# A batch's head in another order: next queries, second values, next keys and the input's transposes moved between half-steps

## The reference

```
x = x + a_alpha * attention(gamma_a * rmsnorm(x) + beta_a)      # 16 heads of width 16, softmax
x = x + f_alpha * (swiglu(gamma_f * rmsnorm(x) + beta_f) @ out_w + out_b)   # 1024 hidden
```

## Time and profile before

| what | value |
|---|---|
| median of 3 runs (lowest, highest) | 949.28 us (947.05, 949.49) |
| the profiled execution's own time | 951.83 us |
| its span, first to last instruction | 950.0 us |
| mean granted clock of PE | 0.985 |
| PE busy | 917.3 us, 97% |
| DVE busy | 746.9 us, 79% |
| ACT busy | 558.1 us, 59% |
| POOL busy | 266.3 us, 28% |

### The profile page before, as it was taken

How to read it: one execution, slowest core, us unless ns; L and a number is a source line. 1 busy time by engine, 2 the same in 40 slices (tenths; PEclk the granted TensorE clock), 3 DMA queues, 4 the chain that set the end, 5 groups by cost and what they waited for, 6 DMA issues and landing times.

```text
span 950.0 us, 19296 instructions
## 1 busy us (share of the span) xinstructions
PE 917.3 (97%) x7128; PEld 671.5 (71%) x7128; DVE 746.9 (79%) x1435; ACT 558.1 (59%) x1162; POOL 266.3 (28%) x255
## 2 busy tenths in 40 slices
PE   6899999999899999999999999999999999999998
PEld 4677777777544677767776786768577777867587
DVE  4798888999788798778778877887797788778253
ACT  5466545544566666566666656665575756566532
POOL 1256432322101032312322322231223223124242
PEclk9999999999999999999999999999999999999999
DMA  9655457443521212132032203303120321120010
GB/s 259 158 136 151 110 146 167 115 119 85 134 87 40 68 65 66 34 106 83 3 91 57 75 13 85 120 6 91 57 74 3 90 68 42 62 63 8 1 29 23
DMA packets 93757, 75.68 MB, mean 80 GB/s; under 512 B 44880, under 2 KB 79768, under 8 KB 93664
## 3 DMA queue, kind: packets, MB, share of 16 engines
q1 hardware_dynamic: 82680, 63.22, 24.2%
q10 hardware_dynamic: 10984, 11.23, 4.4%
HBM read 27.73 MB, written 12.61 MB: 42 GB/s over the span
## 4 chain that ended last, share of the span: by engine, by line
PE 85%; DVE 4%; ACT 3%; SPq 3%; issue 2%; DMA 1%; POOL 1%; ACTq 0%; DVEq 0%; POOLq 0%
PE bank L1405 17%; PE bank L438 17%; PE bank L1118 13%; PE bank L1424 8%; PE bank L1092 8%; PE raw_pair L1026 6%; PE bank L340 3%; PE bank L1410 2%; PE bank L1496 2%; DVE rowmax L1036 1%; PE bank L1668 1%; SPq L929 1%; PE bank L1542 1%; DMA k_stack<-hid 1%; PE bank L1420 1%
## 5 line engine op out<-in xcount | busy, mean ns | idle before, releaser
L1036 DVE TENSOR_REDUCE rowmax<-raw_pair 128x1 f32<-128x512 f32 x488 | 326.1, 684 | 82.3 <-PE raw_pair L1026 80.2
L1107 ACT ACTIVATE probs<-bank 128x512 f32<-128x512 f32 x344 | 197.2, 598 | 126.1 <-PE bank L1092 122.9
L438 PE MATMUL bank<-up_w,xs_part 128*128 128x512 f32 x768 | 199.9, 411 | 6.0 <-POOL xs_part L417 5.9
L1092 PE MATMUL bank<-q_stack,k_stack 50*128 50x512 f32 x480 | 189.1, 410 | 3.7 <-ACT probs L1107 2.2
L1026 PE MATMUL raw_pair<-k_stack,q_stack 48*128 48x512 f32 x456 | 182.0, 412 | 3.3 <-DVE rowmax L1036 2.0
L438 PEld LDWEIGHTS bank<-up_w,xs_part 128*128 128x128 f32 x768 | 139.6, 192 | 40.8 <-POOL xs_part L417 6.9
L1526 POOL TENSOR_TENSOR hid<-scratch,hid 128x512 fp32r<-128x512 f32 x64 | 82.8, 1294 | 227.2 <-ACT hid L1522 227.2
L1107 ACT ACTIVATE third_probs<-bank 128x512 f32<-128x512 f32 x168 | 96.5, 598 | 63.8 <-PE bank L1092 62.4
L1092 PEld LDWEIGHTS bank<-q_stack,k_stack 50*128 50x128 f32 x480 | 85.7, 185 | 39.1 <-ACT probs L1107 18.8
L1405 PE MATMUL bank<-xf_part,gate_w 64*128 64x512 f32 x384 | 112.2, 401 | 1.1 <-DVE xf_part L1288 1.1
L1405 PE MATMUL bank<-xf_part,hidden_w 64*128 64x512 f32 x384 | 111.5, 399 | 0.0
(11 more groups left out here) (215 smaller groups left out, 1646.6 us busy)
## 6 DMA issues: line engine op xcount, KB each, us to landing
q_stack<-hid SPq DMA_DIRECT2D x78, 128.0 KB, 2.8
k_stack<-hid SPq DMA_DIRECT2D x64, 128.0 KB, 3.1
xk<-xT SPq DMA_DIRECT2D x32, 128.0 KB, 3.1
xt<-x_tok SPq DMA_DIRECT2D x32, 128.0 KB, 2.8
x_spill<-x1t ACTq DMA_DIRECT2D x32, 128.0 KB, 2.4
xa_spill<-xa ACTq DMA_DIRECT2D x32, 128.0 KB, 2.3
x_in<-xa_spill SPq DMA_DIRECT2D x8, 512.0 KB, 5.1
x_in<-x_spill SPq DMA_DIRECT2D x8, 512.0 KB, 3.8
```

What stands on the lines that cost most here:

```text
L438: last = nc.tensor.matmul(bank[j][:], xs_part[a][:, m % 2, k, :], up_w[w][:, k, col + j * W:col + (j + 1) * W], start=(i == 0), stop=(i == ...
L1036: nc.vector.reduce_max(rowmax[:, e + RAWS * half:e + RAWS * half + 1], raw_pair[:, half, :], AX.X) \
L1092: nc.tensor.matmul(score_bank[c % 2][:], k_rows[rows, slot, kt * P:(kt + 1) * P], q_rows[rows, slot, :], start=True, stop=True).then_inc(s ...
L1107: nc.scalar.activation(probs_of(n, j), score_bank[c % 2][:], ACT.Exp).then_inc(exp_done, 1)
```

## The change

For the batches with a following one: next queries go to half-step 4, second values to 5, nothing new to 6 (the second values' upper half waits until 7), next keys to 7, with half-step 7's first score in the middle of that piece. Both halves of the input are transposed in 8, between its first and second score, each with one added wait: half 1 for the queries' low part, half 0 for the second values' copy. The second values' copy goes on ACT from 6 to 8, the queries' high copy from 7 to 6, behind 6's exponentials; the queries' low part on DVE goes behind 7's first maximum. The affine copy of half 1 goes from 7 to 8. POOL makes both low halves.

For all loop batches: `mean_dve` goes to half-step 5, `normed_act` to the end of 5 (ahead of 6's exponentials), `normed_dve` to the start of 6, and the bias addition is written three entries later in POOL's program.

```
 # xf_pe
-                if k == 1 and not normed:
+                if not normed and (k == 0) == (c < B - 2):
                     pe.wait_ge(v_free, 2 * (c + 1))
+                elif not normed and k == 1:
+                    pe.wait_ge(pair_free[0], credited(pair_free[0], use[0]))
 # place: ("v",1) 5 -> 6 (5 in the last batch), ("qk",0,0) 6 -> 5
 # chain_free_pe
-            elif p == ("v", 1):
+            elif p == ("v", 1) and b < B - 1:
+                freed(0, at["wo"][0] + 1)
+            elif p in (("v", 1), ("qk", 0, 0)):
                 pe.wait_ge(v_free, 2 * (b - 1) + 1)
...
-                freed(p[2], at["wo"][p[2]] + 1)
+                freed(1, at["wo"][1] + 1)
 # plan
-            table[1:5] = [("v", 0)], [("wo", 0)], [("wo", 1)], [("v", 1)]
+            table[1:4] = [("v", 0)], [("wo", 0)], [("wo", 1)]
             if following:
-                table[5:7] = [("qk", 0, 0)], [("qk", 0, 1)]
+                table[4:8] = [("qk", 0, 0)], [("v", 1)], [], [("qk", 0, 1)]
+            else:
+                table[4] = [("v", 1)]
 # chain_batch_pe
-                excursion_pe(pe, b, h, True, (0,))
+                if following and h == XF_AT:
+                    chain(table[h][0], lambda: excursion_pe(pe, b, h, True, (0,)))
+                else:
+                    excursion_pe(pe, b, h, True, (0,))
...
-                    if table[h] or pending is not None:
+                    if table[h] or pending is not None and not following:
...
                 elif h == XF_AT:
                     second()
-                    xf_pe(pe, b - 1, both(u, at["xf"]), which=(1,) if following else (1, 0))
                     if not following:
+                        xf_pe(pe, b - 1, both(u, at["xf"]))
                         fill_behind_pe(pe, u, at)
                 elif h == FFN_AT:
+                    if following:
+                        xf_pe(pe, b - 1, both(u, at["xf"]))
                     second()
-                    if following:
-                        xf_pe(pe, b - 1, both(u, at["xf"]), which=(0,))
                     values()
 # head_act
-            elif h == 6:
+            elif h == 6 and not following:
                 chain_v_act(act, b, 1)
...
                 squares_act(act, b - 1, h - 4)
-            elif h == 6:
-                normed_act(act, b - 1)
+                if h == 5:
+                    normed_act(act, b - 1)
+            elif h == 6 and following:
+                act.wait_ge(stacked[1], (b + 1) * STACK)
+                qk_act(act, 0, 0, u + at["qk0"][0], chain_bank(b, ("qk", 0, 0)))
 # chain_batch_act, h == FFN_AT
+                    chain_v_act(act, b, 1)
                     exp_act(act, b, 1, 0, 0)
+                    xf_second_act(act, b - 1, both(u, at["xf"]), b + 2)
                     xf_first_act(act, b - 1, both(u, at["xf"]))
                     exp_act(act, b, 1, 0, 1)
 # head_dve: affine_dve, mean_dve behind x2_dve of half-step 5; normed_dve first in 6;
 #           in 7 first() ahead of qk_dve. xf_low_dve is gone.
 # pool_batch
-                    xf_pool(pool, b - 1, both(u, at["xf"]), (1,))
+                    xf_pool(pool, b - 1, both(u, at["xf"]), (1, 0))
+                if ffn and h == FFN_AT + 2:
                     bias_pool(pool, b - 1)
```

More of the change, by code:

```diff
@@ L1283, in xf_dve @@
                 .then_inc(f_in_copied, 1)
[L1285 to L1290, removed]
         def affine_rows_act(act, c, k):
@@ L1334, in cond_seq_kernel, with place @@
         LOWER, UPPER = slice(0, 64), slice(64, 128)
-        def place(p):
+        def place(b, p):
+            if b == B - 1 and p == ("v", 1):
+                return 5
             if p[0] in ("gate", "hidden"):
@@ L1341, in place @@
                 return 8 + 2 * NH + p[1] // HALF
-            return {("qk", 1, 0): 0, ("qk", 1, 1): 1, ("v", 0): 2, ("wo", 0): 3, ("wo", 1): 4, ("v", 1): 5,
-                    ("qk", 0, 0): 6, ("qk", 0, 1): 7, ("xf", 1): 8, ("xf", 0): 9}[p]
+            return {("qk", 1, 0): 0, ("qk", 1, 1): 1, ("v", 0): 2, ("wo", 0): 3, ("wo", 1): 4, ("qk", 0, 0): 5,
+                    ("v", 1): 6, ("qk", 0, 1): 7, ("xf", 1): 8, ("xf", 0): 9}[p]
         PLACES = 8 + 2 * NH + 2
         def chain_bank(b, p):
-            return turn_bank[(PLACES * (b - 1) + place(p)) % 3]
+            return turn_bank[(PLACES * (b - 1) + place(b, p)) % 3]
         def work_bank(c, n, f, spare):
@@ L1824, in head_act @@
                 chain_v_act(act, b, 0)
-            elif h == 6:
+            elif h == 6 and not following:
                 chain_v_act(act, b, 1)
-            elif h == XF_AT and following:
-                act.wait_ge(stacked[1], (b + 1) * STACK)
-                qk_act(act, 0, 0, u + at["qk0"][0], chain_bank(b, ("qk", 0, 0)))
             exps_act(act, b, h)
@@ L1837, in head_act @@
                 squares_act(act, b - 1, h - 4)
-            elif h == 6:
-                normed_act(act, b - 1)
[L1840 to L1843, removed]
+                if h == 5:
[3 more added lines that the diff above has]
+                qk_act(act, 0, 0, u + at["qk0"][0], chain_bank(b, ("qk", 0, 0)))
+            elif h == XF_AT and not following:
+                xf_second_act(act, b - 1, both(u, at["xf"]), b + 1)
+                xf_first_act(act, b - 1, both(u, at["xf"]))
         def chain_batch_act(act, b, u, following):
@@ L1934, in head_dve @@
                     second()
+                else:
+                    affine_dve(dve, b - 1)
+                    mean_dve(dve, b - 1)
             elif h == 6:
+                normed_dve(dve, b - 1)
                 first()
-                affine_dve(dve, b - 1)
-                mean_dve(dve, b - 1)
                 second()
-                normed_dve(dve, b - 1)
             elif h == XF_AT:
+                first()
                 if following:
                     qk_dve(dve, 0, 0, 4 * b + 4, chain_bank(b, ("qk", 0, 0)))
-                first()
                 second()
@@ L1972, in chain_batch_dve @@
                     maxima_dve(dve, b, h, True, 0)
-                if h == FFN_AT:
-                    xf_low_dve(dve, b - 1, both(u, at["xf"]))
                 for half in (1, 0):
```

## The result

The changed kernel takes 937.41 us (median of 4, 934.64 to 938.52) against 949.38 (median of 4, 947.05 to 953.32): ratio 0.9865, 95% interval 0.9825 to 0.9906. Forecast were 936.4 and 0.9864. Three single executions on record (1443, 2176 and 4178 us, one each of three kernels) stand far from all others and are left out of every median and mean here.

The account below looks back on a forecast made before the run. PE, 85% of the chain, was taken as the bound. Five heads at 2.3 us plus 1.4 for batch one and 0 for the last gave 12.9, so 936.4 us as median; 8-in-10 range 932 to 944.5.

Parts of the forecast that it names:

- The sum: Whole loop: 2.3 us in each of batches two to six, 1.4 in batch one, 0 in the last; 12.9 us.
- The early mean: Mean ahead of half-step 6, just behind the squares; scaling starts 1.30 us after it, 1.7 us earlier than before.
- The new wait in half-step 7: Half-step 7's score on PE waits for an exponential queued behind the scaling: a new stall of 1.0 us.
- The queue of ACT as the chain: ACT's queue is full from scaling to the input's last affine copy; gate's low step 9.9 us behind the squares.
- The clock: Half-step 8's value products in batches two to six: clock stays up, 1.85 us instead of 3.43, 1.6 won.
- the first rival: Low clock stays or moves: a head wins only about 0.8 to 1.0 us, time 943 to 944; chance 0.18.
- The term of batch one: First loop batch, no clock to win: low step at 337.3 instead of 338.73, a gain of 1.4 us.
- POOL's low halves: POOL makes both low halves before the gate, 1.27 us each; gate's low step waits for POOL by 0.4.
- The last batch: Only mean and scaling move; PE reaches the transposes about when it did: 0, with 1.6 us either way.
- The slower rival, the ring: ACT and PE handovers delay each other: head 2.1 us later, clock low, 956 us in all; chance 0.08.

Follow-up runs that it names:

- the experiment: The changed kernel with low half 0 by DVE again and the bias addition straight behind GpSimd's low half 1: 938.14 us.
- the last kernel above: The changed kernel with half-step 6's first exponential on ACT and first maximum on DVE ahead of the scaling: 929.46 us, ratio 0.9787.

## Why the prediction was right

*The sum.* 12.9 forecast, 12.8 in the profiled loop, 12.0 between the medians. (In its rivals, 2.3 less 1.6 is 0.7, not 0.8, and six times 1.1 is 6.6, not 6.7; neither changes anything.) That the medians agree as closely (936.4, 937.41) is partly luck, since the changed kernel's own executions lie 4 us apart.

*The early mean.* Forecast 1.7 us earlier scaling with 1.30 between; 1.33 behind the squares. Right. Its worth alone was not forecast: in the old order with DVE's low half it is nothing (948.70), in the new order 3.3 us between the means.

*The new wait in half-step 7.* Forecast 1.0, measured 0.74 in the fourth head and 0.78 to 1.49 in the others. Right, and right that it stands in the place of the wait removed.

*The queue of ACT as the chain.* Squares to transposes 4.7 forecast, 4.8 measured; to the gate 8.15 and 8.3; to the low step 9.9 and 9.7, and the same within 0.1 in all five heads at full clock. That ACT's queue is the bound is shown only in part: the exponential put into its idle time moved the low step by 0.2 of 0.5, then DVE's maximum held PE; with both ahead of the scaling it was 0.7.

*The clock.* Forecast 1.6 a head in batches two to six, all won. In the profiled pair it came so: five low stretches to none, and one in the first batch, where its 1.4 shrank to 0.4 (from squares to squares, 83.93 to 83.53). This is the first rival, in one head of six. The term of batch one was mis-sized by 1.0; the periods of batches two to six fell by 1.9, 2.3, 2.5, 3.3 and 2.5 where 2.3 each was forecast, and batch five made it up. The ground for this term was weak, and here luck helped: batch one, taken as the example of a head that keeps the clock with a thin window, lost it in the profiled execution of the changed kernel and of five of the kernels above, and the changed kernel's profiled execution has the highest clock of its seven (0.995, of 0.989 to 0.995). Over executions the products give 5.7 of 11.7 us to the order and 6.0 to the clock, where the sum had 4.9 and 8.0; by 1.05 to 1.25 us per 0.001 of clock it would be 3.9 to 5.2 and 6.5 to 7.8. The low stretches before are not in fixed heads, as one profile suggested. Why the clock holds more often in the new order was not isolated: late mean, DVE's low half and fillers each change the share, and the moved pieces were never undone alone.

*POOL's low halves.* Forecast 1.27 each and a hold of 0.4; measured 1.27 each and a hold of 0.1. The price was right, but the part earns nothing in the new order, since DVE's took 1.00 there and the low step came as early. The prediction names the rule for a copy; the row that it reads by it, 2.58, is a subtraction with two SBUF inputs, and what the rows show is told at the experiment.

*The last batch.* 0 forecast, +0.3 measured, with its low stretch before and after. At full clock its low step comes 10.2 behind the squares (the kernel with fillers before the keys) and not 11.8.

*The slower rival, the ring.* It needed 2.3 us of delay a head. In the fourth head PE has one wait of 0.25, for a DMA, besides the one of 0.74, and the gate starts 0.2 later behind the squares than forecast.

## What to carry to other kernels

When a short engine queue is the chain, an instruction whose input is early belongs into the idle time in front of the late one, on every engine that the late one stands on; here one exponential and one maximum brought 8 us that the reordering had left, about half of it clock. Price a low clock from many executions, not from the heads of one profile: fillers seemed to hold it in the profiled execution and held it in two of ten. And expect a part that does nothing alone to be held up by another, as the early mean was by DVE's low half in three heads.

## What was not expected of the hardware

The same program's mean granted clock ran from 0.984 to 0.990 in 25 executions, and its time from 944.07 to 954.02. Batches with the same instructions kept 2.4 GHz in one head and ran 3.4 us at 1.2 GHz in the next. With the mean late in the new order three of six heads lost it, though all six had the same wait of 1.7 ahead of the transposes; with the waits of the last kernel above (0.25 to 0.48 each) none of six. A DVE subtraction of 128x512 with both inputs in SBUF took 0.85 to 2.61, and each of 28 ended 0.54 to 0.56 behind the end of the POOL instruction that had started before it; its length tells how early it started, and not what it costs.
